# Delta-rule stage of a transformer kernel: strip transfers behind the inverse's stores, and another order of steps on three engines

## The reference, cut to what matters

```python
g = jnp.exp(-jax.nn.softplus(hidden @ Wfa @ Wfb + dt_bias) * jnp.exp(A_log))   # decay per key
beta = jax.nn.sigmoid(hidden @ Wb)
def step(S, inp):
    qt, kt, vt, gt, bt = inp
    S = S * gt[..., None]
    pred = jnp.einsum('bhk,bhkv->bhv', kt, S)
    delta = (vt - pred) * bt[..., None]
    S = S + kt[..., None] * delta[:, :, None, :]
    o = jnp.einsum('bhk,bhkv->bhv', qt, S)
    return (S, o)
```

## Time and profile before

| | |
|---|---|
| median of 3 runs | 1822.89 us (1809.54 to 1831.44) |
| profiled execution, its own time | 1815.07 us |
| its span | 1813.3 us |
| mean granted TensorE clock | 0.881 |
| TensorE matmul busy | 1519.7 us (84%) |
| VectorE busy | 1239.9 us (68%) |
| ScalarE busy | 1025.5 us (57%) |

### The profile page before, as it was taken

The page is one execution under the profiler, slowest core; times in us unless marked ns, Lnnn a source line. Parts: engine busy times, 40 slices in busy tenths (PEclk is TensorE's granted clock), DMA queues, the critical chain, the costliest instruction groups (busy, mean ns, idle before and its releaser), DMA issues. The chain is left out here.

```text
span 1813.3 us, 41435 instructions
## 1 busy us (share of the span) xinstructions
PE 1519.7 (84%) x14936; PEld 1014.4 (56%) x14936; DVE 1239.9 (68%) x3815; ACT 1025.5 (57%) x2716; POOL 41.2 (2%) x49
## 2 busy tenths in 40 slices
PE   6877889788797678888988888889888988878678
PEld 3534555564454245656666666666666666667435
DVE  5759989856723578777778867877866877864131
ACT  5417878876311556676666756667656656643210
POOL 0000000000000000000000000000000000000000
PEclk9888899889998689899889978989978988968599
DMA  3032000000101211111111111111210211110010
GB/s 149 25 74 69 10 10 4 2 1 1 73 0 27 68 18 44 49 46 27 51 42 31 57 50 17 55 53 22 55 48 16 60 48 18 46 24 14 1 49 23
DMA packets 118312, 67.18 MB, mean 37 GB/s; under 512 B 93648, under 2 KB 107216, under 8 KB 116960
## 3 DMA queue, kind: packets, MB, share of 16 engines
q1 hardware_dynamic: 118112, 64.54, 12.9%
HBM read 51.36 MB, written 6.98 MB: 32 GB/s over the span
## 5 line engine op out<-in xcount | busy, mean ns | idle before, releaser
L1576 DVE SCALAR_TENSOR_TENSOR arena<-arena 128x1024 f32<-128x1024 f32 x144 | 184.6, 1282 | 32.4 <-ACT arena L1151 31.0
L819 PE MATMUL bank<-xt,arena 128*128 128x512 f32 x384 | 195.3, 642 | 5.4 <-ACT arena L1143 4.0
L1654 DVE TENSOR_TENSOR arena<-arena 128x512 f32<-128x512 f32 x224 | 156.2, 697 | 14.6 <-PE bank L872 13.1
L669 PE MATMUL bank<-xt,arena 128*128 128x512 f32 x320 | 143.3, 604 | 3.8 <-DVE arena L1394 3.8
L819 PEld LDWEIGHTS bank<-xt,arena 128*128 128x128 f32 x384 | 72.7, 206 | 72.4 <-issue 70.9
L669 PEld LDWEIGHTS bank<-xt,arena 128*128 128x128 f32 x320 | 60.7, 194 | 87.2 <-issue 87.2
L688 PE MATMUL bank<-arena 128*128 128x256 f32 (+2 forms) x384 | 100.2, 409 | 6.2 <-DVE arena L1394 5.3
L1084 ACT ACTIVATE arena<-arena 128x128 f32<-128x128 f32 x256 | 99.1, 389 | 9.4 <-DVE arena L1504 9.4
L902 PE MATMUL bank<-arena 64*64 64x64 f32 x1024 | 50.4, 258 | 58.0 <-issue 55.2
L872 PEld LDWEIGHTS bank<-arena 128*32 128x32 f32 x5120 | 62.4, 120 | 65.4 <-issue 51.8
L1697 DVE SCALAR_TENSOR_TENSOR arena<-arena,bank 128x128 f32<-128x128 f32 x112 | 38.7, 345 | 87.0 <-PE bank L968 84.9
(11 more groups left out here) (170 smaller groups left out, 3516.3 us busy)
## 6 DMA issues: line engine op xcount, KB each, us to landing
arena<-d_w SPq DMA_DIRECT2D x16, 519.0 KB, 6.4
arena<-beta_scratch SPq DMA_DIRECT2D x16, 512.0 KB, 5.5
arena<-zero_scratch SPq DMA_DIRECT2D x14, 512.0 KB, 4.6
arena<-arena SPq DMA_DIRECT2D x64, 64.0 KB, 2.6
arena<-zero_scratch SPq DMA_DIRECT2D x15, 256.0 KB, 2.9
arena<-w_scratch SPq DMA_DIRECT2D x2, 1376.0 KB, 6.1
arena<-f_idx SPq DMA_DIRECT2D x2, 1072.0 KB, 11.9
w_scratch<-arena SPq DMA_DIRECT2D x2, 1072.0 KB, 4.0
```

The lines of the kernel that those rows point to most:

```text
L669: last = pe.matmul(bank[2 * w + n % 2][0:rows, :], (WU if f < 2 else WU1R)[:, w, k, m * P:m * P + rows], XT[:, k, hf * HALF:(hf + 1) * HAL ...
L819: last = pe.matmul(bank[b][:], DW[:, par, c:c + P], XT[:, k, rhs], start=(k == 0), stop=(k == KC - 1))
L1576: dve.scalar_tensor_tensor(out=CT[:, x], in0=RAW[:, x, 3 - j:3 - j + S], scalar=DW[:, par, tap:tap + 1], in1=CT[:, x], op0=ALU.mult, op1=A ...
L1654: dve.tensor_tensor(kq, kq, left, ALU.mult)
```

## The change

1. On SP, `strips` is no longer a step ahead of `inverse`. Its waits and its four DMAs stand inside `inverse`, between the two stores and the wait for their landing. The waits for `base_step` and `flipped` now come ahead of the wait for `strips_ready`.
2. `PLACE` is written anew for TensorE, ScalarE and VectorE, with the same steps in other places.

```diff
-                def strips(m, par):
-
-                    sp.wait_ge(strips_ready, 2 * m + 2)
-                    wait(sp, full[6], read(6, m - 2, "predict", NT - 1))
-                    for k in range(P // STRIP):
-                        ks = slice(STRIP * k, STRIP * (k + 1))
-                        sp.dma_start(MB[ks, par, :, :, ks], MBC[ks, par]).then_inc(strips_put, 16)
-
                 def inverse(m, par):
 
                     sp.wait_ge(base_step, BASE_STEPS * (m + 1))
                     sp.wait_ge(flipped, m + 1)
...
                     sp.dma_start(blk_x.rearrange("b (i c) -> b i c", i=BLK), ZT).then_inc(inverse_out, 16)
+
+                    sp.wait_ge(strips_ready, 2 * m + 2)
+                    wait(sp, full[6], read(6, m - 2, "predict", NT - 1))
+                    for k in range(P // STRIP):
+                        ks = slice(STRIP * k, STRIP * (k + 1))
+                        sp.dma_start(MB[ks, par, :, :, ks], MBC[ks, par]).then_inc(strips_put, 16)
                     sp.wait_ge(inverse_out, 32 * (m + 1))
...
                     blocks(m, m % 2)
-                    strips(m, m % 2)
                     inverse(m, m % 2)
```

More of the change, by code:

```diff
@@ L63 @@
     "pe": [
[L64 to L78, removed]
+        (0.212, "piece", 7), (0.432, "piece", 2), (0.473, "piece", 3), (0.555, "piece", 1), (0.596, "piece", 0),
@@ L79 @@
+        (2.801, "solve", 4), (2.829, "update", 4), (2.87, "predict", 5), (2.897, "solve", 5), (2.925, "update", 5),
+        (2.979, "predict", 6), (2.993, "solve", 6), (3.034, "update", 6), (3.075, "predict", 7), (3.103, "solve", 7),
+        (3.158, "update", 7), (3.226, "final"), (3.418, "turn_out", 0), (3.692, "turn_out", 1), (3.815, "project", 2),
+        (3.911, "project", 1), (4.116, "project", 0), (4.171, "project", 3),
     ],
     "act": [
-        (0.483, "piece", 7), (0.54, "piece", 2), (0.588, "piece", 3), (0.644, "piece", 1), (0.695, "piece", 0),
@@ L82 @@
[L82 to L91, removed]
+        (0.412, "piece", 7), (0.465, "piece", 2), (0.482, "piece", 3), (0.518, "piece", 1), (0.553, "piece", 0),
@@ new lines @@
+        (0.623, "silu", 1), (0.658, "piece", 6), (0.693, "exp_z"), (0.781, "piece", 4), (0.798, "square", 1),
+        (0.833, "piece", 5), (0.886, "ln_z"), (1.061, "norm", 0), (1.079, "norm", 1), (1.096, "exp_g"), (1.114, "exp_k"),
+        (1.184, "silu", 2), (1.237, "silu", 0), (1.289, "square", 0), (1.377, "turn_v", 1), (1.605, "level", 5, 0),
+        (1.675, "turn_v", 0), (1.746, "flip"), (1.868, "level", 5, 1), (1.904, "gate", 0), (1.939, "gate", 1),
+        (1.956, "level", 6, 1), (1.974, "level", 6, 0), (2.009, "left", 4, 0), (2.044, "left", 4, 1), (2.149, "left", 5, 0),
@@ new lines @@
+        (2.202, "left", 5, 1), (2.254, "keys", 0), (2.272, "left", 6, 0), (2.307, "right", 6, 0), (2.325, "left", 6, 1),
+        (2.36, "solve", 0), (2.395, "keys", 1), (2.447, "update", 0), (2.5, "solve", 1), (2.535, "update", 1),
+        (2.57, "right", 6, 1), (2.588, "solve", 2), (2.64, "update", 2), (2.711, "solve", 3), (2.728, "update", 3),
+        (2.763, "solve", 4), (2.816, "update", 4), (2.851, "solve", 5), (2.921, "update", 5), (2.991, "solve", 6),
+        (3.026, "update", 6), (3.132, "solve", 7), (3.167, "update", 7), (3.219, "final"), (3.342, "rows", 0),
@@ L92 @@
+        (3.43, "rows", 1),
     ],
     "dve": [
[L94 to L101, removed]
-        (1.716, "less", 2), (1.716, "less", 3), (1.734, "less", 4), (1.735, "less", 5), (1.741, "less", 6), (1.745, "less", 7),
```

39 lines of the change are left out of this document (29 added, 10 removed).

## The result

| | before | after |
|---|---|---|
| median of 4 runs | 1816.22 us (1803.75 to 1831.44) | 1715.76 us (1709.24 to 1727.48) |
| profiled execution, own time / span | 1815.1 / 1813.3 | 1727.48 / 1725.7 |
| mean granted clock | 0.881 | 0.917 |

The ratio is 0.948, with a 95% interval of 0.939 to 0.957; that is 95 us. The forecast was 1773 us, with a range of 1740 to 1810. The direction was right; the gain, 49.5 us by the forecast, came out at 100 by the medians.

A forecast was written before the change was run, and what follows sets the result against it. TensorE, nearest to full, was held to idle 58.0 us before `left`, waiting for XX loads. Transfers 40.0 plus clock 13.5 minus order 4 gave 49.5 us off the median 1822.9: 1773 us, own range 1757 to 1790, whole range 1740 to 1810.

The forecast's parts named there:

- SP's part: At the wait before `left 4`: stores ahead of strips start the loads 2.64 us earlier a head, 40.0 us in all.
- Rival B: On SP's queue: strips slow the loads, gain only 0.8 us a head, 13 us, no clock: 1810 us; chance 0.08.
- The clock: TensorE after the wait before `left 4`: shorter waits bring back the full granted clock, worth 13.5 us.
- So 2.7 us, for five slow odd heads: Periods of odd heads: 67.23 us slow against mean 64.5 at full speed, giving 13.5 us.
- For the even heads I find no such difference (8 to 9, slow, takes 64.39, and 10 started late), and count nothing: Periods of even heads: no gain from full clock counted; the range allowed up to 2 us for each of five.
- With 2.64 us less, all but head 0's wait (6.00) come below 2.5: Waits before `left 4`: all but head 0's fall below the boundary, placed between 2.29 and 2.86 us, for full clock.
- The new order: The rewritten step table on three engines: a loss of 0.3 us a head, some 4 us in all.
- I take a gain of 0.2 a head, between 0 and the 1.16 us that level 0 waits now: Before `level 0`: moving `total 1` off the way to `key 2` releases it earlier, 0.2 us a head.
- `turn_v 0` ahead of `predict 2`: On TensorE between level 3 and `predict 2`: 0.60 us more work, costless at full speed, taken as 0.3 us a head.
- C: Rival: clock fully back, even heads included, 40 + 25, and 5 to 15 from the order: 1745 us; chance 0.15.
- A: Rival: saved time becomes TensorE waits at `predict` and `update`; half of the 40, no clock: 1803 us; chance 0.17.
- D's long periods: Rival: clock falls between level 0 and level 3, periods of 71.1 us like head 3's: 1845 us; chance 0.08.

The follow-up runs named there:

- the orders alone: The kernel before with the three new step orders of TensorE, ScalarE and VectorE, SP as before: 1801.81 us, ratio 0.995.
- nothing else changed: The kernel before with six unused 128x256 products in front of TensorE's wait at `left 4 0` in each head: 1789.26 us, ratio 0.988.
- the strips alone: The kernel before with SP's new order (stores, strips, landing), all other step orders as before: 1752.59 us, ratio 0.969.
- the strips and three products: The kernel before with SP's new order plus three unused 128x256 products in front of the wait of `left 4 0`: 1743.14 us, ratio 0.964.
- the pause filled: The kernel before with the three new step orders and six unused 128x256 products in front of `left 4 0`, SP as before: 1762.08 us, ratio 0.967.

## Why the prediction was wrong

- **SP's part: right.** Loads 2.86 us behind level 4 (forecast 2.8), the sum before L902 at 17.4 (18 to 20), and 34 us in E, where the forecast had 37 for heads 1 to 15. Its 2.64 us for head 0 are not seen: that wait is 5.98 us after 6.00, and the start of head 0, 4.0 us earlier here, is 8.3 us earlier with the orders alone, where the transfers are as before. `flip` comes 1.5 us ahead of the tick, as it had to. Rival B is refuted: its 0.8 us a head became 2.3, and the strips delay the series of loads by 0.25 us. By the ring order of the Trainium skill ("DMA: Bandwidth & Descriptors", "Queues, rings and completion order") I had reckoned with its far end; the loads here follow four 64 KB transfers at once and no such delay shows.
- **The clock: right mechanism, term too small.** 13.5 us forecast. 22 to 27 were measured with nothing else changed and five heads still slow, 25 in A with the strips alone, and 40 in A with the strips and three products, where every head but head 0 runs at its full-clock time. Of the 25, 22 lie in odd heads and 3 in even ones; of the 40, 22 and 18. So three things were off.
  - "So 2.7 us, for five slow odd heads" was too small. A shortens by 2.9 to 6.0 us in heads 1, 3, 7, 11 and 13.
  - "For the even heads I find no such difference (8 to 9, slow, takes 64.39, and 10 started late), and count nothing" was wrong. In A the even heads from head 2 on take 14.9 to 16.8 us before and 13.5 in the same order at full clock. I had judged both kinds by whole periods, where a late start of one head hides in the next; the distance from `left 4 0` to `level 0` in each head would have shown it.
  - "With 2.64 us less, all but head 0's wait (6.00) come below 2.5" did not bring the clock back in the even heads: the boundary that I had placed between 2.29 and 2.86 us does not hold. With the strips alone, waits of 1.52 to 2.92 us were followed by a clock of 0.54 to 0.72. It took the new orders, or three products more, to bring it back.

  The Trainium skill's rule that the throttled state is the default ("TensorE: Matmul & The Clock Gate", "What's actually happening"), by which I had priced 25 us more, gave 38.5. A shows 40 at the full clock, the whole kernels 22 to 27 with the clock back in most heads; the kernels with unused products lose 0.4 to 0.6 us a head in E, so which of the two is the net price is open.
- **The new order: the step that failed.** "Sum 0.3 a head lost, 16 heads, some 4 us", with 11 us for what was taken at nothing. Alone it gives 15 us (10 by the ratio), with the pause filled 27, on top of the strips 37 by the medians and 39 by the ratios (18 between the profiled executions). Even its sign was wrong; on top of the strips the 11 us did not reach it by far. The way it failed: the forecast took for granted that the strips alone bring the clock back, and priced the orders without it. Of its terms: "I take a gain of 0.2 a head, between 0 and the 1.16 us that level 0 waits now" was too small. The wait for `key 2` was 9.3 us in the groups of the stage, all of which vanished; at full clock A is 1.1 us shorter in the odd heads and 0.3 in the even ones. "The pairs in `solve`, `update`, `predict` trade one gap for another of the same kind; nothing" does not fit B, which falls from 14.83 to 14.03 with the orders alone; which of the moved steps does it is not shown. `turn_v 0` ahead of `predict 2` cost, but by another way than forecast: through the wait at `predict 3` and the half-speed `piece 4` (D +0.6).
- **The parts were added.** By the medians 64 + 15 is 79, not 100. Much of the difference is the clock: the strips bring the waits of the even heads to 1.5 to 2.9 us, which was not enough; the new orders bring them to at most 1.2, and the clock comes back. With the orders alone the waits stay at 2.0 us and more, and it does not. A smaller part may be the orders' own: among even heads (from head 2 on) with a clock of 0.50 over the 6 us from `left 4 0`, A is 16.4 to 16.8 us before and 17.0 and 17.1 with the orders alone, so there they gain nothing, while at full clock they gain 0.3 and 1.1. As I read it, at the low clock TensorE sets A, and VectorE's shorter way to `key 2` is not on the path. The forecast had written down that "VectorE sets the pace in `key` to `level 0`" and used it only to lower the clock's term, not to raise the order's. That the two together are all of the 21 us is not shown.
- **The rivals.** C (clock fully back, 5 to 15 us from the order, 1745) had both mechanisms and still undersized them. A did not happen. VectorE's waits for the products of `predict` (L1686, now L1684) did grow from 26.1 to 48.5 us in the stage, but this comes from the orders and not from the time saved at `left`: with the strips alone they are 28.2, with the orders alone 57.6. Those for the products of `update` (L1697, now L1695) fell from 72.5 to 21.8, to 31.6 with the strips alone. D's long periods were a mark of the low clock: with the strips alone, where the odd heads have it back, they are gone.
- **Still open:** whether the worths of the three engines' orders add up; how the 21 us divide; what in B takes back the gain at `piece 4`; why the unused products delay `left 4 0` by 0.4 us; why one wait of some 2.5 us keeps the clock and another of 1.5 does not.

## What to carry to other kernels

When two edits both shorten the waits of TensorE, do not price them apart and add: the first may leave the waits just too long for the full clock, and the second bring it back, and then two gains are more than their sum. Measure the worth of a clock over a stretch of the same steps, head by head, and not over periods that end in a wait. Before a step is moved ahead of a piece of independent work, ask which copy that work was hiding.

## What the runs showed of the hardware

- Unused work in a wait paid: six products of 256 columns, 2.75 us in head 8, in each head made the whole kernel 27 us faster by the medians (22 by the ratio, 9 to 36).
- The length of the last wait alone did not decide the clock behind it. In the kernel before, waits of 1.69 to 2.29 us were followed by 1.00 over the next 6 us. With the strips alone one of 1.58 us was too, but those of 1.52, 1.54 and 1.63 us by 0.57 to 0.72. Behind the unused products waits of 2.61 and 2.63 us were followed by 1.00, one of 2.53 us by 0.59.
- A granted clock fell behind short waits too, and not each time. In the changed kernel waits of 1.38 or 1.39 and 0.22 us, with a few short products between them, stand ahead of `piece 4` in ten periods: in five it ran at about half speed, in five at full speed. With 0.79 or 0.80 and 0.22 us, in 13 periods of the kernel with `turn_v 0` moved, it was always at full speed.
- Four 64 KB transfers issued just ahead of 16 loads on the same queue cost those loads 0.25 us in issue, and landed in the same 2.6 us as before.
